# Gathering expert rows tile by tile through a row map, in place of sixteen scatters ahead of all tiles, and applying the gates after the tiles

## The reference

```python
x = x + attention(layernorm(x), ctx, ctx, mask)      # 16 heads over up to 6404 context rows
h0 = layernorm(x)
probs = softmax(h0 @ gate_w.T)                        # 8 experts
topk_probs, topk_idx = top_k(probs, 2)
h = gelu(h0 @ w1[:, e, :].T + b1[e])                  # per chosen expert e, 512 wide
y = h @ w2[:, e, :].T + b2[e]
x = x + sum over the two choices of y * topk_probs
```

## Time and profile before

| | |
|---|---|
| median of 3 runs | 335.9 us (335.01, 335.9, 337.93) |
| the profiled execution | 335.63 us |
| its span, first to last instruction | 333.9 us |
| mean granted PE clock | 0.916 |
| PE busy | 260.5 us, 1855 instructions |
| DVE / ACT / POOL busy | 170.1 / 230.8 / 84.7 us |

### The profile page before, as it was taken

The page is one execution under the profiler, slowest core; times in us unless marked ns, Lnnn a source line. Parts: engine busy times, 40 slices in busy tenths (PEclk is TensorE's granted clock), DMA queues, the critical chain, the costliest instruction groups (busy, mean ns, idle before and its releaser), DMA issues.

```text
span 333.9 us, 6252 instructions
## 1 busy us (share of the span) xinstructions
PE 260.5 (78%) x1855; PEld 130.2 (39%) x1856; DVE 170.1 (51%) x420; ACT 230.8 (69%) x364; POOL 84.7 (25%) x138
## 2 busy tenths in 40 slices
PE   2587866499999999989899999986484169999940
PEld 2464535122222221212222222235473169999940
DVE  4638966044544535353545454438751047676622
ACT  4366564389999999999999999961794024555520
POOL 8899002100000000000000000402057504444430
PEclk9999895599999999999999999997789559999995
DMA  6999790001101010101001010199201170111115
GB/s 195 381 273 399 291 206 17 5 23 23 34 5 39 0 39 12 28 12 28 18 22 26 14 32 7 39 377 276 36 33 48 48 183 26 32 33 34 31 32 187
DMA packets 29091, 29.57 MB, mean 89 GB/s; under 512 B 15357, under 2 KB 22929, under 8 KB 28944
## 3 DMA queue, kind: packets, MB, share of 16 engines
q1 hardware_dynamic: 27456, 26.21, 26.1%
q0 software_dynamic: 1616, 3.13, 3.2%
HBM read 21.62 MB, written 7.45 MB: 87 GB/s over the span
## 4 chain that ended last, share of the span: by engine, by line
issue 27%; PE 26%; ACT 20%; DVE 7%; DMA 7%; another core or an unknown queue 4%; POOL 3%; SPq 2%; ACTq 1%; DVEq 1%; POOLq 1%
ACT w2T L995 9%; ACT arenaB L995 9%; PE bank L1278 6%; DMA mask_u<-in_mask_BxSxS_bk_dram 5%; PE bank L1397 5%; PE bank L1260 5%; PE bank L1405 3%; DVE arenaB L900 2%; PE bank L1345 2%; PE bank L1169 1%; DMA arenaA<-ys_dram 1%; DVE arenaB L906 1%; PE bank L1355 1%; DVEq L895 1%
## 5 line engine op out<-in xcount | busy, mean ns | idle before, releaser
L717 DVE TENSOR_TENSOR arenaA<-bank,arenaA 128x512 f32<-128x512 f32 x80 | 55.2, 690 | 76.4 <-PE bank L1278 76.4
L995 ACT ACTIVATE arenaB<-bank 128x1024 f32<-128x1024 f32 x80 | 77.5, 1021 | 8.3 <-PE bank L1260 6.2
L995 ACT ACTIVATE w2T<-bank 128x1024 f32<-128x1024 f32 x80 | 76.7, 1030 | 1.3
L1260 PE MATMUL bank<-qS,keys 64*128 64x512 bf16 x324 | 63.2, 389 | 10.1 <-ACT w2T L995 5.7
L1025 ACT ACTIVATE mask_u<-bank,arenaB 128x128 f32<-128x128 f32 x92 | 26.2, 368 | 39.7 <-PE bank L1397 39.7
L1260 PEld LDWEIGHTS bank<-qS,keys 64*128 64x128 bf16 x324 | 15.4, 93 | 97.1 <-ACT w2T L995 49.4
L1278 PE MATMUL bank<-arenaB,vcur 128*32 128x512 f32 x320 | 42.6, 605 | 1.0
L1278 PE MATMUL bank<-w2T,vcur 128*32 128x512 f32 x320 | 42.6, 605 | 0.0
L411 POOL CAST keep<-flags 128x1 f32 x11 | 2.1, 187 | 141.0 <-DVE arenaC L628 140.3
L478 POOL DMA_INDIRECT ys_dram<-arenaB,mask_u x23 | 22.2, 964 | 36.3 <-DVE arenaB L906 36.3
L1397 PE MATMUL bank<-arenaB 128*128 128x128 f32 x184 | 27.4, 296 | 2.8 <-DVE arenaB L892 2.5
(11 more groups left out here) (301 smaller groups left out, 325.7 us busy)
## 6 DMA issues: line engine op xcount, KB each, us to landing
mask_u<-in_L_ffn_w_dram SPq DMA_DIRECT2D x2, 2048.0 KB, 10.6
mask_u<-in_mask_BxSxS_bk_dram SPq DMA_DIRECT2D x6, 560.5 KB, 16.0
ctx_sb<-in_ctx_dram SPq DMA_DIRECT2D x3, 768.0 KB, 13.2
qS<-qparts_dram SPq DMA_DIRECT2D x4, 448.0 KB
mask_u<-in_mask_BxSxS_bk_dram SPq DMA_DIRECT2D x6, 240.0 KB, 11.6
keys_in<-kparts_dram SPq DMA_DIRECT2D x40, 32.0 KB
mask_u<-in_mask_BxSxS_bk_dram SPq DMA_DIRECT2D x1, 1121.0 KB, 8.4
xs_dram<-w1T SPq DMA_DIRECT2D x2, 520.0 KB, 16.8
```

The source lines that it names most:

```text
L717: nc.vector.tensor_tensor(a, bank[:, 4 + k % 2, :], a, ALU.add).then_inc(s["ac"], 1)
L995: nc.scalar.activation(probs[u % 8], bank[:, 2 * (u % 2):2 * (u % 2) + 2, :].rearrange("p a b -> p (a b)"), ACT.Exp, scale=SCALE).then_inc ...
L1260: last = mm(bank[:, 2 * (u % 2) + a, :], keys[rows, g, :], qS[rows, g, cols], start=not hides, stop=True, tile_position=(64 * a, 0))
```

## The change

The normalized rows are written once, plainly, to `xn_dram`. A row map says for each slot which row it holds. It is made by sixteen 0/1 products on PE: `in_tile` says which place within its tile a pair has, `by_tile` which tile, times the partition number plus one (`pcol`) or the column number (`ccol`). DVE turns the product's two values into `x_row` (what to gather) and `y_row` (where to store; spare numbers for empty slots). POOL gathers tile j's rows from `xn_dram` by `x_row`, four ahead of all tiles, and tile j+4 behind the store of tile j. The scaling by the gate moves behind the tiles: `gates` is applied when `back` is added. ACT makes the rows (all eight columns, once) before it loads the Exp table. The gates' turns and the b2 products move into the tile loop, and so do DVE's parts of them.

```diff
-ROW = D + 2
-XS_CUTS = [(0, 2), (2, 8), (8, 16), (16, NT)]
+AHEAD = 4
...
@@ SP
             sp.dma_start(w2raw, w2).then_inc(s["w2_in"], 16)
-            sp.wait_ge(s["fill"], 2)
-            for b in range(3):
-                sp.dma_start(xs_dram.rearrange("(j s) c -> s j c", s=P)[:, b:NT:3, :],
-                             fill[:, b:b + 1, :].broadcast_to([P, len(range(b, NT, 3)), ROW])).then_inc(s["xs_fill"], 16)
-            sp.wait_ge(s["scat"], 16 * 2 * QT)
-            for k, (j0, j1) in enumerate(XS_CUTS):
-                sp.dma_start(xs_sb[:, j0:j1, :], xs_dram.rearrange("(j s) c -> s j c", s=P)[:, j0:j1, :]).then_inc(xs_in[k], 16)
+            sp.wait_ge(s["cq_sb"], 2 + QT)
+            sp.dma_start(xn_dram.rearrange("(p t) d -> p t d", t=QT), xn2).then_inc(s["xn_out"], 16)
...
@@ POOL
-            pool.wait_ge(s["xs_fill"], 48)
-            pool.wait_ge(s["slot"], 8)
-            pool.wait_ge(s["rdy"], 2)
-            for k in range(2):
-                for t in range(QT):
-                    c = k * QT + t
-                    pool.wait_ge(s["cq_sb" if k else "ln2"], t + 1 + 2 * k)
-                    nc.gpsimd.indirect_dma_start(xs_dram, bass.IndirectOffsetOnAxis(ap=slots[:, c:c + 1].bitcast(U32), axis=0),
-                                                 rows[k][:, t, :], None).then_inc(s["scat"], 16)
+            def gather(j):
+                nc.gpsimd.indirect_dma_start(xs_sb[:, j, :], None, xn_dram,
+                                             bass.IndirectOffsetOnAxis(ap=x_row[:, j:j + 1].bitcast(U32), axis=0)).then_inc(xs_in[j % AHEAD], 16)
+
+            pool.wait_ge(s["xn_out"], 16)
+            pool.wait_ge(s["map_sb"], 11)
+            for j in range(AHEAD):
+                gather(j)
             for j in range(NT):
-                pool.wait_ge(s["yacc"], j + 2)
-                nc.gpsimd.indirect_dma_start(ys_dram, bass.IndirectOffsetOnAxis(ap=xs_sb[:, j, ROW - 1:ROW].bitcast(U32), axis=0),
+                pool.wait_ge(s["yacc"], j + 1)
+                nc.gpsimd.indirect_dma_start(ys_dram, bass.IndirectOffsetOnAxis(ap=y_row[:, j:j + 1].bitcast(U32), axis=0),
                                              ysb[:, j % 3, :], None).then_inc(y_out[j % 3], 16)
+                if j + AHEAD < NT:
+                    pool.wait_ge(xs_in[j % AHEAD], 16 * (j // AHEAD + 1))
+                    gather(j + AHEAD)
...
@@ DVE, behind the slots (the old rows, gates and b2 sum go from here)
+            dve.wait_ge(s["tconst"], 14)
+            map_step(nc.vector.tensor_scalar(tile_i, slots, 7, None, ALU.logical_shift_right), 1)
+            map_step(nc.vector.tensor_copy(tile_f, tile_i), 2)
+            map_step(nc.vector.scalar_tensor_tensor(within, tile_f, -float(P), slots_f, ALU.mult, ALU.add), 3)
+            nc.vector.tensor_tensor(in_tile[:, 0:QT, :], cc(within, P)[:, 0:QT, :], iota_q.rearrange("p (a q) -> p a q", a=1).broadcast_to([P, QT, P]), ALU.is_equal)
+            map_step(nc.vector.tensor_tensor(hot_tile, cc(tile_f, NT), iota_j.rearrange("p (a j) -> p a j", a=1).broadcast_to([P, 2 * QT, NT]), ALU.is_equal), 4)
+            nc.vector.tensor_scalar(by_tile[:, :, 0, :], hot_tile, pcol, None, ALU.mult)
+            nc.vector.tensor_tensor(by_tile[:, :, 1, :], hot_tile, cc(ccol, NT), ALU.mult).then_inc(s["map_in"], 1)
+            nc.vector.tensor_tensor(in_tile[:, QT:2 * QT, :], cc(within, P)[:, QT:2 * QT, :], iota_q.rearrange("p (a q) -> p a q", a=1).broadcast_to([P, QT, P]), ALU.is_equal).then_inc(s["map_in"], 1)
...
+            dve.wait_ge(s["map_ps"], 1)
+            row_step(nc.vector.tensor_copy(row_f[:, 0:2, 0:NT], bank[:, 2, 0:2 * NT].rearrange("p (a j) -> p a j", a=2)), 1)
...
+            row_step(nc.vector.tensor_copy(y_row, column), 11)
...
@@ DVE, tiles and end
-            def gated(j):
+            def result(j):
...
-                nc.vector.tensor_scalar(ysb[:, j % 3, :], bank[:, 4 + j % 2, 0:P], xs_sb[:, j, D:D + 1], None, ALU.mult).then_inc(s["yacc"], 1)
+                nc.vector.tensor_copy(ysb[:, j % 3, :], bank[:, 4 + j % 2, 0:P]).then_inc(s["yacc"], 1)
...
+                if j == 2:
+
+                    for k in range(2):
+                        dve.wait_ge(s["gT_ps"], k + 1)
+                        nc.vector.tensor_copy(epi_e[:, 512 * k:512 * k + 512], bank[0:E, 6 + k, :]).then_inc(s["gT_sb"], 1)
+                if j == 5:
+                    dve.wait_ge(s["b2ps"], 1)
+                    nc.vector.tensor_tensor(x2, x2, bank[:, 6:8, :].rearrange("p a (t d) -> p (a t) d", d=D), ALU.add).then_inc(s["b2ps"], 1)
...
-                nc.vector.tensor_tensor(x2, x2, back[k].rearrange("p (t d) -> p t d", d=D), ALU.add).then_inc(s["fin"], 1)
+                for t in range(QT):
+                    nc.vector.scalar_tensor_tensor(x2[:, t, :], back[k][:, t * D:(t + 1) * D], gates[:, k, t:t + 1], x2[:, t, :], ALU.mult, ALU.add).then_inc(s["fin"], 1)
...
@@ ACT (the same eight passes for rows[1] go from among the weight copies, with the wait for xs_fill)
             nc.scalar.activation(ln[:, 1, :], ln[:, 0, :], ACT.Sqrt).then_inc(s["gtexp"], 1)
+            act.wait_ge(s["sqrt2"], 7)
+            for t in range(QT):
+                nc.scalar.activation(xn2[:, t, :], x2[:, t, :], ACT.Identity, scale=ln[:, 3, t:t + 1], bias=ln[:, 4, t:t + 1]).then_inc(s["cq_sb"], 1)
             nc.scalar.preload_act_table(ACT.Exp)
...
@@ PE
             expert_weights(0, E)
+            pe.wait_ge(s["map_in"], 6)
+            pe.wait_ge(s["slot"], 8)
+            for c in range(2 * QT):
+                last = mm(bank[:, 2, 0:2 * NT], in_tile[:, c, :], by_tile[:, c, :, :].rearrange("p a j -> p (a j)"), start=(c == 0), stop=(c == 2 * QT - 1))
+            last.then_inc(s["map_ps"], 1)
             expert_weights(E, 2 * E)
...
             def slots_turn(j):
-                if j in first:
-                    pe.wait_ge(xs_in[first[j]], 16)
+                pe.wait_ge(xs_in[j % AHEAD], 16 * (j // AHEAD + 1))
...
                 down(j)
+                if j == 1:
+                    gates_turn()
+                if j == 4:
+                    b2_products()
```

More of the change, by code:

```diff
@@ L162, in build @@
         x2 = after[:, 0:1024].rearrange("p (t d) -> p t d", d=D)
-        rows = [arenaA[:, ROW * QT * k:ROW * QT * (k + 1)].rearrange("p (t c) -> p t c", c=ROW) for k in range(2)]
-        xn2 = rows[0][:, :, 0:D]
+        xn2 = arenaA[:, 0:1024].rearrange("p (t d) -> p t d", d=D)
+        in_tile = arenaA[:, 1024:2048].bitcast(BF16).rearrange("p (c q) -> p c q", c=2 * QT)
+        by_tile = arenaA[:, 3104:3472].bitcast(BF16).rearrange("p (c a j) -> p c a j", c=2 * QT, a=2)
+        hot_tile = arenaA[:, 3472:3840].rearrange("p (c j) -> p c j", c=2 * QT)
         back = [arenaA[:, 2080:3104], after[:, 4096:5120]]
@@ L207, in build @@
         oh_b = after[:, 1752:1784].bitcast(BF16)
+        iota_q = after[:, 5888:6016]
+        iota_j = after[:, 6016:6016 + NT]
+        pcol = after[:, 6040:6041]
+        ccol = after[:, 6048:6064]
+        spare = after[:, 6064:6064 + NT]
+        tile_i = after[:, 6088:6104].bitcast(I32)
+        tile_f = after[:, 6104:6120]
+        within = after[:, 6120:6136]
+        row_f = after[:, 6136:6136 + 4 * 24].rearrange("p (a j) -> p a j", a=4)
+        x_row = after[:, 6232:6232 + NT].bitcast(I32)
+        y_row = after[:, 6256:6256 + NT].bitcast(I32)
+        gates = after[:, 6280:6296].rearrange("p (k t) -> p k t", k=2)
         maskw = mask_u8[:, :, :].bitcast(I32)
@@ L227, in build @@
         mask_in = [[None] + [sem(f"mask_in{b}_{t}") for t in range(1, QT)] for b in range(len(MASK_CUTS))]
-        xs_in = [sem(f"xs_in{k}") for k in range(len(XS_CUTS))]
+        xs_in = [sem(f"xs_in{k}") for k in range(AHEAD)]
         y_out = [sem(f"y_out{k}") for k in range(3)]
@@ new lines, in _ @@
+            for b in range(3):
+                nc.gpsimd.iota(spare[:, b:NT:3], [[0, len(range(b, NT, 3))]], base=PAIRS + b * P + QT, channel_multiplier=1,
+                               allow_small_or_imprecise_dtypes=True).then_inc(s["tconst"], 1)
+            def gather(j):
+                nc.gpsimd.indirect_dma_start(xs_sb[:, j, :], None, xn_dram,
+                                             bass.IndirectOffsetOnAxis(ap=x_row[:, j:j + 1].bitcast(U32), axis=0)).then_inc(xs_in[j % AHEAD], 16)
@@ new lines, in _ @@
+            row_step(nc.vector.scalar_tensor_tensor(row_f[:, 3, 0:NT], row_f[:, 2, 0:NT], -float(QT), column, ALU.mult, ALU.add), 4)
+            row_step(nc.vector.tensor_scalar(row_f[:, 3, 0:NT], row_f[:, 3, 0:NT], -float(QT), 0.0, ALU.add, ALU.max), 5)
+            row_step(nc.vector.tensor_copy(x_row, row_f[:, 3, 0:NT]), 6)
+            row_step(nc.vector.scalar_tensor_tensor(column, row_f[:, 2, 0:NT], float(S - QT), column, ALU.mult, ALU.add), 7)
+            row_step(nc.vector.scalar_tensor_tensor(part, part, 0.0, spare, ALU.is_equal, ALU.mult), 8)
@@ new lines, in _ @@
+            row_step(nc.vector.tensor_tensor(column, column, part, ALU.add), 9)
```

(14 more changed lines are left out.)

88 lines of the change are left out of this document (44 added, 44 removed).

## The result

The changed kernel takes 347.62 us (median of four, 345.41 to 349.8), the kernel before beside it 335.78 (335.01 to 337.93): a ratio of 1.0313, 95% interval 1.0256 to 1.0369. It is slower, as forecast, but by 11.8 us between the medians where 4.4 were forecast. The profiled execution took 345.41, with a span of 343.4; it was the fastest of the four.

The account below looks back on a forecast made before the run. Bound: a hole ahead of the expert tiles, then 23 tiles that PE and DVE fill. Last scatter at 324.5 + 11.6 + 1.5 + 1.0 = 338.6, +4.7 on the span, so 340.3 us; range 331 to 349.

Parts of the forecast that it names:

- The start: Ahead of the expert tiles: scatters, fills and loads go, so first products come at 257.0, 13.5 us earlier.
- ACT's chain: Start: eight Identity passes, Exp table load, exponential, sixteen weight copies, then DVE's staging; first products at 255.9 to 258.6.
- the map's chain: Start: DVE's and PE's row-map steps give index columns at 252.6, first gather at 252.7, first products at 257.0.
- The loop: Tile stage: turn, scatter, gather behind it and landing close over two tiles; period 3.14+L, 5.84 us where it was 4.18.
- L: Tile stage: a gather's landing time after issue, taken as 2.7 us, nearer the scatter's 2.23 than the upper bound 3.2.
- term for turns and b2: Inside the tiles: gate turns, b2 products, two DVE copies and a sum, no longer hidden under scatters, cost 1.0 us.
- Turn to scatter: Tile stage, part of the two-tile period: 1.95 us before, 1.88 after a copy replaces the scaled copy.
- Gates at the end: After the last scatter: two 1024-element sums become two groups of eight products; 1.5 us more, bounds 0.7 and 2.2.
- No change (L of 2.2): Rival on the tile stage: landing as short as the scatter's, turns and b2 wholly hidden; 334.3 us, chance 0.25.
- Faster, gathers ahead: Rival on the tile stage: gathers stay ahead, period stays 4.18, the start's 13.5 us come through; 323.6 us, chance 0.13.
- Clearly slower by late signals behind b2's sum: Rival inside the tiles: PE's late signals hold DVE's queue, 9.1 us in place of 1.0; 348.4 us, chance 0.2.
- port rule: Tile stage: a gather could wait for a 0.43 us weight copy nine times, 3.9 us, 344; in range, not sum.

Follow-up runs that it names:

- set 5: Earlier kernels rerun side by side, no late signals: changed kernel 346.32, eight gathers ahead 331.51, kernel before plus unread 128-row gathers 337.41, deeper buffers in two-deep order 329.55.
- set 1: Changed kernel with eight gathers ahead 342.71; down products before turn 346.42; empty slots fetching different rows 345.21; gate turns and b2 left out 348.44.
- set 4: Changed kernel, seven gathers ahead, three-deep buffers: two-deep order 331.63; three-deep order with empty slots spread 330.98. Kernel before plus unread 64-row gathers 337.50.
- set 2: Kernel before plus an unread 128-row gather behind every second scatter 343.53; eight gathers ahead with stores on SyncE 330.23, or with loads on SyncE 327.86.

## Why the prediction was right on the direction and wrong on the size

**The start: right.** First products at 257.76 for 257.0, first scatter 262.86 for 262.7, gather 4 at 264.18 for 264.0. That the scatter is nearer than the products is luck: from the one to the other it took 5.10 for 5.74, and the two errors cancel. ACT's chain and the map's chain came within a microsecond of their sums.

**The loop: the mechanism right, its length not.** The step that failed is the size of L, the gather's issue to its turn: 2.7 "nearer the scatter" for every tile, and with it the loop as one chain of tiles of equal landings. The runs show 3.0 on average along the even tiles and 3.3 along the chain that set the time. PE's turns wait for gathers, over two tiles, as written. But tile 22's turn came at 324.87, not 319.3: 58.13 us for nine periods from tile 4's turn at 266.74, where 52.6 were forecast. Followed along the even tiles in the changed kernel's profile, the other 5.6 us are these (1.0 of them could be what the forecast had as its term for turns and b2).

- L, the term of 2.7: gather's issue to turn was 27.12 in nine, 3.01 each, +2.8. Tiles 6 to 12, 16 and 18 had 2.55 to 2.90; tiles 14, 20 and 22, with 93, 128 and 128 slots that read one row, took 3.24, 3.57 and 3.92. The bounds 2.2 to 3.2 were those of a gather of distinct rows. That the map sends every empty slot to row 0 stood in the diff, and I gave it no price.
- Turn to scatter, the term of 1.88: 19.0 in nine, 2.11 each, +2.1 against it. In set 5 a clean turn took 1.84. Late signals before the results of tiles 2, 12 and 14 made some 1.2 us of the excess. The longest, 2.73 for tile 6's result, was none: DVE came late from b2's sum and GpSimd had gather 9 ahead of the scatter (0.9), and tile 10's scatter waited for the queue in the same way (0.3).
- Scatter's start to gather's start, 12.0 for nine times 1.26: +0.7.

In set 5 there were no late signals, and the loop from tile 4 to tile 22 took 59.14, not less. In their place PE's granted clock was in part at its lower level of 1.2 GHz, 0.74 on average from 279 to 283 and 0.66 from 290 to 294, behind waits for gathers, and eight records of up products took 1.92 instead of 1.16:

```profile
279.14 1.92 PE L1453 MATMUL bank<-arenaB 128*128 128x128 f32 x8
```

In the first profile of the changed kernel the clock was full from 271 on, so this is not always paid; it is one more way in which the waits cost more than their own length.

**PE's order ties odd and even tiles.** I priced the loop as if each parity went by itself. The chain of set 5 goes through gathers 5, 7, 9 and 11, then 14, 16, 18, 20 and 22, that of the first profile through 4, 6, 11, 14, 17, 20 and 22: it changes parity with whichever gather is late. So it picks up the slow landings of both parities, tiles 7 and 11 (126 and 108 slots that read one row) among them, and issue to turn on the chain is 3.3 on average in both profiles. Two of these slow landings, tile 17's 3.79 in the first profile and tile 5's 3.77 in set 5, have no such row to blame; with eight gathers ahead the same tiles landed in 2.6 and 2.5, and what held them is open.

**Gates at the end, b2 inside the tiles.** Scatter 22 to the end of the span took 13.4, for 11.6 + 1.5. The two groups of eight took 2.2 each (4.3 for sixteen was the estimate). The 1.0 for turns and b2 is neither shown nor refuted: b2's products held the turn of tile 7 to 277.3, the sum then found its turn on DVE without a wait, and leaving all out made the tail 0.9 shorter, less than tails of one kernel differ by.

**The last step.** 329.99 for the last scatter against 325.5 (324.5 and the 1.0) is +4.5; the end +0.3; what lies around the span 2.0 for 1.7; and the median of the runs lies 2.2 over the profiled one. 340.3 + 4.5 + 0.3 + 0.3 + 2.2 = 347.6. The last of these is the spread of executions and no part of the mechanism.

**The rivals.** No change (L of 2.2): refuted, the shortest landing of a gather in set 5's changed kernel was 2.47. Faster, gathers ahead: it didn't happen at four, and at eight it gave 331.5, not 323.6: GpSimd's two issues a tile made 2.32 us a tile where 2.09 was the pace before (5 us over 22 tiles), and that run's first scatter lay 2.4 later, 2.0 of it before the row map. That GpSimd's work "is over 4.18 too, but under the loop" was right, and is the bound behind it. Clearly slower by late signals behind b2's sum: no such wait stood there; that its 348.4 lies near the measured 347.62 is chance. Late signals are real, but cost about 1.2 here along the even tiles, and the time without them was no better.

**The two rules that were weighed.** The fit of the Trainium skill, "DMA: Bandwidth & Descriptors", section "Anatomy of one DMA — SWDGE (gpsimd) path", gave 2.15: in set 5's changed kernel most scatters landed at 2.23 to 2.35, gathers at 2.47 to 3.72. For gathers the two differ, and the measurement decides. (The prediction calls "no change" the second rival beside this fit; in its list it is the first.) On the port rule of the Trainium skill ("SBUF — State Buffer", "Who interferes with whom"): in the changed kernel GpSimd's indirect issues grew from 964 to 1014 ns on average, 0.05 each, not a copy's 0.43. With fills on GpSimd, both sides grew, and the kernel was 3 to 6 us slower; that the one is the cause of the other is likely, not shown.

## What to carry to other kernels

A prefetch depth counts in the queue that issues it: "four ahead" was two tiles of slack, because each gather stood behind a scatter, that behind a result, and PE had a later turn ahead of that result. Write the loop down with its landing time, and price the landing for the worst index list, with repeated rows, not for the mean. With the loop open (eight ahead) the change is worth 1.6% in set 5 (0.9837), though in set 1, with late signals, it was 1.6% slower (1.0159). Seven ahead with more buffers gave 0.9895 in set 4 and 0.9772 in set 5; the intervals overlap with that of eight ahead, so a gain from the buffers isn't shown. And run a kernel's variants side by side more than once before a cause is named: set 2 agreed with my theory in all three runs, and the one of them that was run again lost its effect.

## What the runs showed of the hardware

- The same kernel with eight gathers ahead took 342.71 in one set and 331.51 in another, while the kernel before stood at 336.42 and 336.53. In the slower set PE's signals came 0.4 to 3.9 us after the recorded (modelled) ends of products (the longest: a turn's end at 296.38, its copy at 300.31); in the other there was next to none. The kernel before has them too, under its scatters, where they cost nothing. What in a machine or a moment makes them wasn't found; that in set 2 they went with dense indirect DMAs is shown, that these cause them is not.
- In set 5's changed kernel a gather of 64 KB landed 2.47 to 2.86 us after its issue, but for two of 3.35 and 3.72; with 93 to 128 slots reading one row it was 3.22 to 3.72.
- Two fills on GpSimd, 0.64 us each, at every second tile made the kernel before 1.3% slower (1.0128); a plain load or a gather issued at the same place, nothing that can be measured (1.0020, 1.0019 in set 5), though in set 2, with late signals, the gather's kernel was 2.2% slower (1.0217).
